# Graph attention on one core: units taken in pairs, group sums laid out two blocks ahead, window addresses read eight at a time

## What is computed

```python
qkv = (h @ Wqkv + bqkv).reshape(N, 3, H, DH)        # N=625, H=8, DH=64
logits = einsum('ehd,ehd->eh', q[src], k[dst])      # 20000 edges, sorted by dst
a = logits + dist_attn + path_attn
e = exp(a - segment_max(a, dst)[dst])
sa = e / segment_sum(e, dst)[dst]
agg = segment_sum(v[src] * sa[:, :, None], dst)     # then agg @ Wo + bo, layer norm, feed forward
```

## Time and profile before

| | us |
|---|---|
| median of three runs | 824.91 |
| the profiled execution's own time | 826.6 |
| its span in the profile | 825.0 |
| attention stage, from the first one-hot table to the last collect | 97.4 to 323.3 |

### The profile page before, as it was taken

The page is one execution under the profiler, slowest core; times in us unless marked ns, Lnnn a source line. Parts: engine busy times, 40 slices in busy tenths (PEclk is TensorE's granted clock), DMA queues, the critical chain, the costliest instruction groups (busy, mean ns, idle before and its releaser), DMA issues. The chain is left out here.

```text
span 825.0 us, 14610 instructions
## 1 busy us (share of the span) xinstructions
PE 700.9 (85%) x4978; PEld 550.0 (67%) x4978; DVE 530.6 (64%) x1109; ACT 418.2 (51%) x689; POOL 162.0 (20%) x240
## 2 busy tenths in 40 slices
PE   3987766776777764999999999999999999999993
PEld 2664333444555443479999679878889899888792
DVE  6737775788778543544422636338888788888854
ACT  4235333575656653373333543227666676676640
POOL 6341376455544103000000000400000000000022
PEclk9999965999989977999999999999999999999998
DMA  8633545656565581700001040957677677766124
GB/s 263 169 78 74 102 109 165 168 151 178 152 176 166 169 298 28 266 1 1 1 0 62 16 153 1 324 206 257 201 226 235 222 240 237 268 224 227 69 63 144
DMA packets 104157, 125.63 MB, mean 152 GB/s; under 512 B 32402, under 2 KB 70060, under 8 KB 103564
## 3 DMA queue, kind: packets, MB, share of 16 engines
q1 hardware_dynamic: 96955, 115.06, 43.9%
q0 software_dynamic: 5600, 6.54, 3.6%
q10 hardware_dynamic: 1520, 3.01, 1.6%
HBM read 94.91 MB, written 29.67 MB: 151 GB/s over the span
## 5 line engine op out<-in xcount | busy, mean ns | idle before, releaser
L2150 PE MATMUL ps<-xT,w_hi 128*128 128x480 f32 (+7 forms) x512 | 110.1, 337 | 2.3 <-DVE hT L1969 2.2
L2150 PEld LDWEIGHTS ps<-xT,w_hi 128*128 128x128 f32 x512 | 82.0, 189 | 9.9 <-DVE hT L1969 4.0
L1045 PE MATMUL ps<-onehot,group_weights 128*32 128x314 bf16 x1272 | 63.8, 347 | 26.3 <-POOL group_weights L926 8.6
L946 DVE TENSOR_SCALAR onehot<-iota_h,windows 128x628 bf16<-128x628 f16 x212 | 78.8, 433 | 4.1 <-PE ps L1045 4.0
L1955 DVE TENSOR_TENSOR w_lo<-weights_far,w_hi 128x1024 fp32r<-128x1024 f32 x64 | 77.9, 1219 | 2.5 <-ACT w_hi L2065 2.2
L2152 PEld LDWEIGHTS ps<-xT,w_lo 128*128 128x128 f32 x512 | 73.5, 190 | 1.6
L2152 PE MATMUL ps<-xT,w_lo 128*128 128x240 f32 (+7 forms) x512 | 74.5, 268 | 0.0
L1045 PEld LDWEIGHTS ps<-onehot,group_weights 128*32 128x32 bf16 x1272 | 38.6, 113 | 52.1 <-issue 28.4
L2065 ACT ACTIVATE w_hi<-weights_far 128x1024 fp32r<-128x1024 f32 x64 | 67.1, 1051 | 0.0
L168 POOL DMA_DIRECT2D windows<-window_scratch x104 | 58.8, 568 | 36.9 <-issue 30.9
L2175 PE MATMUL ps<-w_hi,hidden 128*128 128x512 f32 (+3 forms) x176 | 62.2, 405 | 2.7 <-DVE hidden L1979 1.9
(11 more groups left out here) (309 smaller groups left out, 1544.6 us busy)
## 6 DMA issues: line engine op xcount, KB each, us to landing
weights_far<-in_L_ffn_w SPq DMA_DIRECT2D x64, 512.0 KB, 5.8
sums_scratch<-sums_out SPq DMA_DIRECT2D x53, 314.0 KB
weights_near<-in_L_ffn_w SPq DMA_DIRECT2D x32, 512.0 KB, 3.4
sums_in<-sums_scratch SPq DMA_DIRECT2D x40, 309.1 KB
weights_near<-in_L_gnn_W SPq DMA_DIRECT2D x4, 1024.0 KB, 6.5
weights_near<-in_L_ffn_sw SPq DMA_DIRECT2D x8, 512.0 KB, 5.1
weights_near<-in_L_gnn_Wqkv SPq DMA_DIRECT2D x3, 1024.0 KB, 7.8
weights_ff<-in_L_gnn_W SPq DMA_DIRECT2D x1, 3072.0 KB, 13.2
```

The lines of the kernel that those rows point to most:

```text
L946: dve.tensor_scalar(onehot[w % 3][:, j, :], iota_h, windows[:, w % RING, j, 1:2], None, ALU.is_equal)\
L1045: last = pe.matmul(psW(w)[r, a, :], R[w % 3][:, j, :, part], onehot[w % 3][:, j, a * SH:(a + 1) * SH], start=part == 0, stop=part == 2)
L2150: pe.matmul(both(bank, cap), w[u % 2][0][:, c, cut], xT(r)[:, c, :, :], start=c == 0, stop=False)
```

## The change

Units are taken in pairs on every engine, and a pair gets 8/3 blocks (3, 3, 2, ...). DVE computes both units' weights, then the two next maxima with the one-hot tables of two blocks between them, and lays out blocks two ahead of PE; a block's mask now comes ahead of its one-hot tables. `sums_in` has four places. SP and POOL load two neighbouring blocks each in turn (SP those with w % 4 of 0 and 1, POOL 2 and 3) and read the addresses of both at once; POOL reads ahead of its wait for the mask. SP looks 8 and 7 blocks ahead, POOL 6 and 5, and six blocks are loaded before the stage. SP asks for the rows of both next units together, after the last store of a pair. The number of blocks, units, matmuls, copies and bytes stays the same. The diff without its unchanged parts:

```diff
@@ -69,7 +69,7 @@
 AHEAD = 6
-LOADED = 4
+LOADED = 6
 SPARE_BLOCKS = 3
@@ -144,27 +144,52 @@
-def blocks_by(unit):
-    return min(WB, window_blocks(0) + SPARE_BLOCKS + (13 * unit + 9) // 10)
-def unit_blocks(unit):
-    return range(blocks_by(unit), blocks_by(unit + 1)) if unit < UNITS_ALL else range(0)
+def blocks_by(pair):
+    return min(WB, window_blocks(0) + SPARE_BLOCKS + (8 * pair + 2) // 3)
+def pair_blocks(pair):
+    return range(blocks_by(pair), blocks_by(pair + 1))
+def laid_out(pair):
+    return range(min(WB, blocks_by(pair) + 2), min(WB, blocks_by(pair + 1) + 2))
...
-def load_groups(nc, eng, engine, w, tab, rec2_d, windows, g_in):
-    _, starts = nc.values_load_multi_w_load_instructions(tab[0:1, REL + GW * w:REL + GW * w + GW], engines=[engine], min_val=0,
+PAIRS = UNITS_ALL // 2
+def by_pool(w):
+    return w % 4 >= 2
+def place_at(w):
+    return [b for b in range(LOADED, 2 * WB) if by_pool(b)][w // 2], [b for b in range(LOADED, 2 * WB) if not by_pool(b)][w // 2]
+def load_starts(nc, engine, w, tab):
+    n = min(2 * GW, GROUPS - GW * w)
+    _, starts = nc.values_load_multi_w_load_instructions(tab[0:1, REL + GW * w:REL + GW * w + n], engines=[engine], min_val=0,
                                                          max_val=CHUNK * REC2)
+    return starts
+def load_groups(eng, w, starts, rec2_d, windows, g_in):
...
-        frm = region[bass.ds(starts[j], P * REC2)] if k else region[0:P * REC2]
+        frm = region[bass.ds(starts[GW * (w % 2) + j], P * REC2)] if k else region[0:P * REC2]
@@ -419,8 +444,10 @@
             sp.wait_ge(windows_stored, 16)
-            for w in range(0, LOADED, 2):
-                load_groups(nc, sp, mybir.EngineType.SP, w, tab, rec2_d, windows, g_in)
+            for w in range(LOADED):
+                if not by_pool(w):
+                    starts = load_starts(nc, mybir.EngineType.SP, w, tab) if w % 2 == 0 else starts
+                    load_groups(sp, w, starts, rec2_d, windows, g_in)
             sp.dma_start(wo[:, :, :], Wo.rearrange("(c p) n -> p c n", p=P)).then_inc(wo_in, 16)
...
@@ -808,7 +837,7 @@
-        sums_in = [sb(f"sums_in{i}", [P, SRC]) for i in range(3)]
+        sums_in = [sb(f"sums_in{i}", [P, SRC]) for i in range(4)]

@@ -835,7 +864,7 @@
     out_done = [sem(f"sums_out{i}") for i in range(3)]
-    units_in = [sem(f"units_in{i}") for i in range(3)]
+    units_in = [sem(f"units_in{i}") for i in range(4)]
@@ -858,41 +887,44 @@
         with sp.If(longest < CHUNK + 1):
-            def load(w):
-                if w < WB and w % 2 == 0:
-                    wait_past(sp, windows_stored, stored_for(w))
-                    window_free(sp, w)
-                    load_groups(nc, sp, mybir.EngineType.SP, w, tab, rec2_d, windows, g_in)
-            def blocks(ws):
-                for w in ws:
-                    load(w + AHEAD)
-                    sp.wait_ge(w_copied, w + 1)
-                    sp.dma_start(sums_d[w, :, :], sums_out[w % 3]).then_inc(out_done[w % 3], 16)
+            starts = None
+            def block(w):
+                nonlocal starts
+                nxt = place_at(w)[1]
+                if w % 2 == 0 and nxt < WB:
+                    starts = load_starts(nc, mybir.EngineType.SP, nxt, tab) if nxt % 2 == 0 else starts
+                    wait_past(sp, windows_stored, stored_for(nxt))
+                    window_free(sp, nxt)
+                    load_groups(sp, nxt, starts, rec2_d, windows, g_in)
+                sp.wait_ge(w_copied, w + 1)
+                sp.dma_start(sums_d[w, :, :], sums_out[w % 3]).then_inc(out_done[w % 3], 16)
...
                         sp.wait_ge(out_done[i], 16 * len(range(i, window_blocks(tile), 3)))
-                wait_past(sp, summed, u - 2)
+                wait_past(sp, summed, u - 3)
...
-                sp.dma_start(sums_in[u % 3][0:TILE, :], rows[g0:g0 + TILE // GD, 0:GD, h, :]).then_inc(units_in[u % 3], 16)
-            for w in range(LOADED, AHEAD):
-                load(w)
-            blocks(range(window_blocks(0) + 1))
+                sp.dma_start(sums_in[u % 4][0:TILE, :], rows[g0:g0 + TILE // GD, 0:GD, h, :]).then_inc(units_in[u % 4], 16)
+            for w in range(window_blocks(0) + 1):
+                block(w)
             unit_rows(0)
             unit_rows(1)
-            blocks(range(window_blocks(0) + 1, leading))
-            for u in range(UNITS_ALL):
-                if u + 2 < UNITS_ALL:
-                    assert blocks_by(u) >= window_blocks((u + 2) // H)
-                    unit_rows(u + 2)
-                blocks(unit_blocks(u))
-                if UNITS_ALL - 10 <= u < UNITS_ALL - 2 and u % 2 == 0:
-                    load_w1(sp, W1, w_near, [(u - UNITS_ALL + 10) // 2], w1_in)
+            for w in range(window_blocks(0) + 1, leading):
+                block(w)
+            for q in range(PAIRS):
+                if q + 1 < PAIRS:
+                    assert blocks_by(q) >= window_blocks((2 * q + 2) // H)
+                    unit_rows(2 * q + 2)
+                    unit_rows(2 * q + 3)
+                for w in pair_blocks(q):
+                    block(w)
+                if PAIRS - 5 <= q < PAIRS - 1:
+                    load_w1(sp, W1, w_near, [q - PAIRS + 5], w1_in)
         sp.wait_ge(windows_stored, 16 * len(ROUNDS))
@@ -914,19 +946,20 @@
             pool.wait_ge(consts, 6)
-            def load(w):
-                if w < WB and w % 2:
-                    wait_past(pool, windows_stored, stored_for(w))
-                    window_free(pool, w)
-                    load_groups(nc, pool, mybir.EngineType.Pool, w, tab, rec2_d, windows, g_in)
+            starts = None
             for w in range(WB):
+                nxt = place_at(w)[0]
+                if w % 2 == 0 and nxt < WB and nxt % 2 == 0:
+                    starts = load_starts(nc, mybir.EngineType.Pool, nxt, tab)
                 pool.wait_ge(masked, w + 1)
...
-                load(w + AHEAD - 1)
+                if w % 2 == 0 and nxt < WB:
+                    wait_past(pool, windows_stored, stored_for(nxt))
+                    window_free(pool, nxt)
+                    load_groups(pool, nxt, starts, rec2_d, windows, g_in)
         pool.wait_ge(ff_vec_in, 80)
@@ -938,19 +971,22 @@
-            def group_weights(w):
+            def masks(w):
                 dve.wait_ge(g_in[w % RING], groups_in(w))
-                wait_past(dve, w_ready, w - 2)
-                for j in range(GW):
-                    dve.tensor_scalar(onehot[w % 3][:, j, :], iota_h, windows[:, w % RING, j, 1:2], None, ALU.is_equal)\
-                       .then_inc(oh_ready, 1)
                 k0 = GW * w % GPB
...
+            def onehots(w):
+                wait_past(dve, w_ready, w - 2)
+                for j in range(GW):
+                    dve.tensor_scalar(onehot[w % 3][:, j, :], iota_h, windows[:, w % RING, j, 1:2], None, ALU.is_equal)\
+                       .then_inc(oh_ready, 1)
@@ -961,10 +997,10 @@
-                dve.wait_ge(units_in[u % 3], 16 * (u // 3 + 1))
+                dve.wait_ge(units_in[u % 4], 16 * (u // 4 + 1))
@@ -974,20 +1010,33 @@
-            for w in range(2):
-                group_weights(w)
-            guards(0)
-            for w in range(2, blocks_by(1)):
-                group_weights(w)
-            for u in range(UNITS_ALL):
-                weights(u)
-                if u % 2 == 0 and u:
-                    collect(u // 2 - 1)
-                if u + 1 < UNITS_ALL:
-                    guards(u + 1)
-                for w in unit_blocks(u + 1):
-                    group_weights(w)
-            collect(UNITS_ALL // 2 - 1)
+            for w in range(leading + 2):
+                masks(w)
+                if w in (1, 2):
+                    guards(w - 1)
+                onehots(w)
+            for q in range(PAIRS):
+                ws = list(laid_out(q))
+                weights(2 * q)
+                if q:
+                    collect(q - 1)
+                weights(2 * q + 1)
+                for w in ws[0:1]:
+                    masks(w)
+                if q + 1 < PAIRS:
+                    guards(2 * q + 2)
+                for w in ws[0:1]:
+                    onehots(w)
+                for w in ws[1:2]:
+                    masks(w)
+                if q + 1 < PAIRS:
+                    guards(2 * q + 3)
+                for w in ws[1:2]:
+                    onehots(w)
+                for w in ws[2:]:
+                    masks(w)
+                    onehots(w)
+            collect(PAIRS - 1)
@@ -1016,17 +1065,25 @@
-            for w in range(2):
+            for w in range(leading):
                 copied(w)
-            exps(0)
-            for w in range(2, leading):
-                copied(w)
-            for u in range(UNITS_ALL):
-                norm(u)
-                if u + 1 < UNITS_ALL:
-                    exps(u + 1)
-                keep(u)
-                for w in unit_blocks(u):
+                if w in (1, 2):
```

(34 more changed lines are left out.)

8 lines of the change are left out of this document (5 added, 3 removed).

## The result

The changed kernel takes 814.89 us (median of 7 runs, 812.27 to 819.18) against 824.91 (7 runs, 822.4 to 828.7) on the same chip: ratio 0.9878, 95% interval 0.9842 to 0.9914. It is 10 us faster, and the interval leaves no doubt that it is faster. The profiled execution took 812.27 us, span 810.5. So the two spans differ by 14.5 us, the medians by 10.

A forecast was written before the change was run, and what follows sets the result against it. SP's issue queue was taken as fullest before the change, the PE-ACT-DVE loop as setting pairs after it. Gains of 5 (head), 13 (middle), 6 (next four pairs) and 2 (end) make 26 us: 799 us, range 785 to 815.

The forecast's parts named there:

- The reads of eight: Address reads on SP: one read of eight takes 3.4 us against 4.2 for two of four.
- the middle: Units 0 to 29, which still have blocks to make: 128 us against 140.7, 13 us gained.
- The end: After the last four pairs, up to the last collect: 9 us against 10.9, 2 us gained.
- The next four pairs: First four pairs of the last ten units, without blocks: 26 us against 32.1, 6 us gained.
- The signs of being wrong: DVE waiting for sums_in in most pairs, load-free pairs over 8.2 us at full clock, or units 0-29's mean clock under 0.92.
- the loop: Chain through PE, ACT and DVE closing a pair: 8.2 us with three blocks, 7.25 with two; late rows make 8.3.
- SP stays the bound: Rival, chance 0.2: eight-value reads cost two of four and in-order waits add 12% to 8.4 us a pair; about 814 us.
- The saving of the long reads: Eight-address reads save SP 0.7 us per four blocks, taking its work from 8.4 to 7.9 us a pair.
- The sum of 23.6: SP's issues in three pairs: sums reads 5.3, stores 3.8, window loads 7.6, address reads 6.9 us; 7.9 a pair.
- The head: Leading blocks before the first weights: two extra preloaded blocks hidden, two loads fewer, sums reads 5 us earlier (range 0 to 8).
- the gain should arrive whole: Stage's end: what follows starts behind a barrier, unchanged, so all 26 us should reach the program's time.
- The clock: PE in units 0 to 29: half clock half as frequent as before, 8% of the time, costing 3 us.

The follow-up runs named there:

- experiment 3: Changed kernel with the bounds check of each address read cut on both queues, SP and GpSimd; 791.69 us, ratio 0.9565 to the kernel before.
- experiment 9: Changed kernel with the bounds check of address reads cut on SP's queue alone, GpSimd keeping it; 794.0 us, ratio 0.9634 to the kernel before.
- Experiment 4: Changed kernel with reads of four addresses again, one per block loaded; 816.45 us, ratio 0.9858 to the kernel before.
- experiment 8: Kernel before with only the change's loads (six blocks loaded ahead, two in turn per queue, eight-address reads), units one at a time; 826.08 us, ratio 1.0004.
- experiment 5: Kernel before, with its four-address reads cut of the bounds check and nothing else changed; 813.46 us, ratio 0.9832.
- experiment 1: Changed kernel with the five feed-forward bias and norm vector loads asked for in pair 12, ahead of W1; 810.71 us, ratio 0.9793 to the kernel before.

## Why the prediction was wrong

**Right.** The reads of eight: 3.28 to 3.46 us in six of seven where 3.4 was worked out, half as many. Waits for rows bunched at every third pair, behind an eight-value read, and PE's waits for one-hot tables gone from the middle (3.6 us before; of 11.1 us in front of weight loads 2.3 are left). The end: 1.8 us for 2. The next four pairs: 4.9 for 6.

**The signs of being wrong.** The mean clock of the middle fell under 0.92 (0.87), and the waits for rows were not shorter than 9.6 us in seven but 20.5 in eight, counted in the same way. The reads of sums started at 132.7, where "near 130" was written.

**The step that failed first: loop and SP were compared, not coupled.** The prediction had SP at 7.9 us a pair and the loop at 8.3 and let the longer one set the time, with 0.4 us for late rows. But SP waits in order, for ACT's copies, for stores to land and for a free place in `sums_in`, and DVE waits for rows behind SP. Measured were 26.3 us for three pairs (192.26 to 218.53; the three before them took 27.3) where 24.9 were forecast and 23.6 was the work on SP. Of the 26.3 us SP waited 2.6, which leaves 23.7 of work: the work was sized rightly, and its waits came on top of it instead of vanishing in a longer loop. That time spent waiting in one pair is not made up in the next, because that one brings a read of 3.4 us and two window loads at once, is the likely reading; no run takes it apart.

Over the twelve pairs in which SP still loads windows (137.3 to 246.6) SP waited 10.3 us of 109.3, before 10.1 of 115.1 (139.5 to 254.6): 91% not waiting in both. The queue is as full as it was, at 9.1 us a pair where 8.3 were forecast. (SP's waits for copies add up to 17.2 us over the whole middle, 18.3 before, but 13.7 and 11.4 of them stand at its end, where it has few windows or none left to load.) Experiments 3 and 9 are the other half of the account: cut 14.6 us from SP, and the middle falls by 16.3; SP then waits 14% of these pairs in the one and 19% in the other.

**The rival came out by luck.** "SP stays the bound" (chance 0.2) had the right bound and the right reason, in-order waits on top of the queue's work. But its 814 us is not built as the result is: it took reads of eight to cost as much as two of four (they took 3.4 us for 4.2) and put the waits on the old 8.4 us a pair, so it gave the middle 2 to 3 us, where 8.1 were measured. That the total agrees is owed to the 4.8 us lost at the barrier, which it had not either. With its 12% put on the 23.6 us of the changed queue it would have had 26.4 us for three pairs, which is what was measured.

**The saving of the long reads.** The sum counted 0.5 us a pair for them (8.4 to 7.9). Experiment 4 shows that this saving never reached the time: with reads of four the middle is 132.9 us for 132.6.

**Sizes on SP.** The sum of 23.6 took a window DMA at 0.48 us from one undisturbed row; the mean was 0.52 (34.4 us for 66). That is 0.7 us in three pairs at most; how much of the middle's miss (8.1 us gained for 13) is size and how much waiting, the runs don't split further.

**The loop and DVE.** The prediction closed a pair at 8.2 us (three blocks) or 7.25 (two), 7.9 in the mean, and put DVE under it at 7.3 us a pair. With SP relieved the pairs take 8.0 us in the mean (experiment 9), but this agreement does not show the loop: DVE is busy 8.1 to 8.6 us of the three-block pairs, and with both queues relieved three pairs with eight blocks took 22.9 us (experiment 3, from 154.35), less than the loop's 23.65. DVE's 7.3 us was a mean; a three-block pair already held 8.7 us of DVE's work before (148.1 to 159.2).

**The head: 2.2 us for 5.** The two extra blocks were to be hidden and two loads fewer to count. The second half came, the first did not:

```profile
94.90 5.04 SPq L138 DMA_DIRECT2D window_scratch<-edge_parts  x2
132.68 1.88 SPq L911 DMA_DIRECT2D sums_in<-sums_scratch  x2
```

From the end of the stores of `edge_parts` to the reads of sums SP took 37.6 us before (97.70 to 135.33) and 32.7 after (99.94 to 132.68), 4.9 us less; but these two stores took 5.04 us to issue where they had taken 2.00, so SP entered the head 2.2 us later. Why they took longer with the extra window loads in front of them was not looked into. In experiment 8 the same loads gave 1.2 us. The head too runs at SP's pace: without the check on SP it ends 7.7 us earlier (129.6 for 137.3), with that on GpSimd cut it does not. ACT stood 17.4 us of the head at waits for stores to land (nine waits), before mostly at waits for PE.

**"What follows the stage starts behind a barrier and is unchanged, so the gain should arrive whole."** This cost 4.8 us, as much as the middle's error (4.9). The barrier waits for all engines, and only the chain to the last collect was followed. GpSimd's additions and its drain of 7.9 us were already the last to arrive before (327.7 against the collect's 323.3); a gain in front of them only shows if they move as well. They moved less: the vectors, asked for 19 us earlier, landed 11.6 us after the request instead of 3.4, behind the rows and W1.

**The clock.** The prediction expected half clock half as often (8% of the middle). The mean was 0.87, so 26% of it. It stands mostly in the two-block pairs (and the first), which took 6.8 us all the same for a forecast of 7.25 at full clock. In experiment 9 the same pairs ran at 1.00 and took 6.8 us again: the half clock in them cost nothing and was no part of the error. With SP relieved the clock of the middle is back at 0.97 to 0.99.

**The sum.** By the profiles: 2.2 + 8.1 + 4.9 + 1.8 up to the last collect, less 4.8 lost at the barrier, is 12.3 us for the stage (forecast 5 + 13 + 6 + 2 = 26); the last 2.2 of the 14.5 between the spans are scatter in the rest of the program. The medians keep 10.

## What to carry to other kernels

A queue that issues in order and waits for the loop it feeds is longer than its work: add its waits to its work before comparing, and if the sum is near the loop's length, call the queue the bound. Count what a register value costs in it; here the bounds check of the addresses, invisible in every engine's busy time, was worth 3% of the program, and a shorter order of work only paid in full once it was gone. Before saying that a gain at a barrier arrives whole, look which engine reaches the barrier last, and move that one's inputs along.

## What was not expected of the hardware

Nearly all of the register work per value is the check: beside the load of 1.05 us a read of eight spends 0.28 to 0.30 us a value with it, and 0.04 without (1.35 less 1.05, over eight). In reads of four it is the same 0.26 us a value (2.08 us with it in the kernel before, 1.04 without in experiment 5). The load grows with the count: on SP 0.27 us for one value, 0.72 for four, 1.05 for eight; on GpSimd 0.33 for four, 0.58 for eight. The Trainium skill (DMA: Bandwidth & Descriptors, "Latency and other measured facts") gives a register load a floor of about 600 ns; the runs show 0.27, 0.33 and 0.58 us below it.

GpSimd's drain at a barrier ended 7.9 us after its last addition in both kernels and in experiment 1, where ACT's took 14 ns and DVE's 0.1 us. With the additions done 37 us earlier, it cost nothing (experiment 1). Why it takes that long was not looked into.
